# Starting a lane's next block under the old one's tail, and ScalarE steps ordered by activation table, in a four-layer graph kernel

## What is computed

```python
x = _layernorm(x + attention_gather_scatter(x, edge_attr, src, dst, ...))        # layer 0
x = _layernorm(x + L1(x, ...))                                                    # layer 1
x = _layernorm(x + segment_sum(x[col] * edge_attr[:, None], row) @ W.T + b)       # layer 2
x = _layernorm(x + segment_sum(value[:, None] * x[col], row))                     # layer 3

def L1(x, ...):
    att = segment_softmax(x[src] @ att_w[:D] + x[dst] @ att_w[D:], dst)
    messages = att[:, None] * (alpha * phys + (1.0 - alpha) * neur)
    h = _layernorm(gelu(segment_sum(messages, dst)) + x, ln1_g, ln1_b)
    m = gelu(h @ mlp_w1.T + mlp_b1) @ mlp_w2.T + mlp_b2
    return _layernorm(m + h, ln2_g, ln2_b)
```

## Time and profile before

| | us |
|---|---|
| median of 3 runs | 3338.48 (3337.09 to 3351.1) |
| the profiled execution | 3352.47 |
| its span in the profile | 3350.7 |
| busy: TensorE, VectorE, ScalarE, GpSimd | 2159.2, 1627.2, 1632.0, 2055.5 |

### The profile page before, as it was taken

How to read it: one execution, slowest core, us unless ns; L and a number is a source line. 1 busy time by engine, 2 the same in 40 slices (tenths; PEclk the granted TensorE clock), 3 DMA queues, 4 the chain that set the end, 5 groups by cost and what they waited for, 6 DMA issues and landing times. The chain is left out here.

```text
span 3350.7 us, 28393 instructions
## 1 busy us (share of the span) xinstructions
PE 2159.2 (64%) x9124; PEld 1081.8 (32%) x9124; DVE 1627.2 (49%) x3065; ACT 1632.0 (49%) x2292; POOL 2055.5 (61%) x1609
## 2 busy tenths in 40 slices
PE   6885777687787888888885744778777730012221
PEld 3432333265333336334333633333332210001210
DVE  5873899837878673443332676332233310012221
ACT  4763566434677672777773333656567720001110
POOL 6888888600488810466657888688800048788887
PEclk9997898769999896999997656888899965555555
DMA  2221222106322211244347342111111101112221
GB/s 57 63 67 43 54 56 53 48 21 191 89 46 43 43 37 47 79 104 106 105 102 160 82 110 69 44 37 38 37 52 38 38 23 14 14 31 57 62 56 26
DMA packets 251594, 204.24 MB, mean 61 GB/s; under 512 B 182627, under 2 KB 192167, under 8 KB 251446
## 3 DMA queue, kind: packets, MB, share of 16 engines
q1 hardware_dynamic: 164998, 154.80, 16.3%
q0 software_dynamic: 83200, 47.29, 8.7%
q10 hardware_dynamic: 3248, 0.34, 0.1%
HBM read 133.83 MB, written 79.64 MB: 64 GB/s over the span
## 5 line engine op out<-in xcount | busy, mean ns | idle before, releaser
L810 PE MATMUL ps<-wk 127*64 127x125 f32 x1200 | 121.0, 367 | 559.0 <-DVE wk L795 558.0
L2172 POOL DMA_INDIRECT stab<-wk,rank_i x200 | 243.1, 1215 | 313.5 <-issue 247.8
L483 ACT ACTIVATE b_s<-ps,vec 128x512 f32<-128x512 f32 (+1 forms) x444 | 297.1, 682 | 125.7 <-PE ps L480 71.4
L2169 POOL DMA_INDIRECT u<-x2tab,dpos_i x200 | 278.0, 1390 | 79.6 <-issue 77.8
L2169 POOL DMA_INDIRECT u<-x3tab,src_i x200 | 258.4, 1292 | 72.3 <-issue 72.3
L2169 POOL DMA_INDIRECT u<-in_x_dram,dst_i x200 | 263.9, 1320 | 61.0 <-issue 57.6
L2169 POOL DMA_INDIRECT u<-in_x_dram,src_i x200 | 249.3, 1246 | 73.5 <-issue 69.2
L810 PEld LDWEIGHTS ps<-wk 127*64 127x64 f32 x1200 | 96.3, 191 | 580.7 <-DVE wk L795 576.7
L2172 POOL DMA_INDIRECT out_dram<-e_c,dst_i x72 | 89.4, 1242 | 309.2 <-issue 309.2
L840 ACT ACTIVATE e_a<-ps 128x500 f32<-128x500 f32 x75 | 44.0, 586 | 456.7 <-PE ps L810 452.3
L2169 POOL DMA_INDIRECT e_b<-x0tab,dpos_i x72 | 91.7, 1274 | 244.0 <-issue 244.0
(11 more groups left out here) (416 smaller groups left out, 5653.5 us busy)
## 6 DMA issues: line engine op xcount, KB each, us to landing
b_s<-in_x_dram SPq DMA_DIRECT2D x98, 256.0 KB
out_dram<-b_gl SPq DMA_DIRECT2D x98, 256.0 KB
wk<-dlist SPq DMA_DIRECT2D x50, 500.0 KB
wk<-slist SPq DMA_DIRECT2D x50, 500.0 KB
u<-stab SPq DMA_DIRECT2D x25, 510.0 KB
x2none<-b_gl SPq DMA_DIRECT2D x25, 250.0 KB
wk<-x2none SPq DMA_DIRECT2D x25, 240.0 KB
x2tab<-wk SPq DMA_DIRECT2D x25, 240.0 KB
```

The source lines that it names most:

```text
L483: return nc.scalar.activation(b_s[l][:, 0:w], (pA, pB)[n][l][:, 0:w], ACT.Abs_reciprocal_sqrt, bias=col(EPSV))
L810: last_a = nc.tensor.matmul(e0[64 * (k % 2):64 * (k % 2) + 64, P * (k // 2):P * (k // 2) + P], msg[n % 2][0:P + 2, D * k:D * k + D], sr[n ...
L2169: pool.indirect_dma_start(out=o, out_offset=None, in_=tab, in_offset=at(ix), **kw).then_inc(s, 16)
L2172: pool.indirect_dma_start(out=tab, out_offset=at(ix), in_=a, in_offset=None, bounds_check=rows_n - 1, oob_is_err=False).then_inc(s, 16)
```

## The change

**The lane.** A dense block's x is now loaded into the second half of `b_gl` and already after `w2` of the lane's previous job (`mlp_pe`), the transposes `t` go to pB, `c` to pA and `j` to pB. So `t` waits only for the lane's last reciprocal root (`rstds`), `u` (or `x`) for the old block's `rows` (`rows_ps`), and `c` (`a`, `s`) for its `out` (`rows_out`). In the plan `-lane` moves from `out` to `r4` (source, destination) or `r5` (dense).

**The plan.** Square roots become a table of their own (3) and steps in no table keep what is loaded. ScalarE looks 1.5 us ahead (`SAME_TABLE`): among the steps that can begin by then, those that need no table change come first, whatever their rank. `GRACE` is .1 instead of .2, copies `act|dve` count each engine's slowness and table change, and `HOLD` starts no dense block in two stretches (before the first source group, and from late in layer 1's carried rows to the third destination group). No arithmetic changes.

```diff
+        LAST_MLP = MLP.format(" -lane")
+        MLP = MLP.format("")
...
-            unit(("src", g), 1, "t pe .5 +lane;x act 1.2;s pe 2.2;r act .7;h dve .9;" + MLP + "rows pe .5;out act|dve .7 -lane",
+            unit(("src", g), 1, "t pe .5 +lane;x act 1.2;s pe 2.2;r act .7;h dve .9;" + LAST_MLP + "rows pe .5;out act|dve .7",
...
-                 "sq5 act .75;j5 pe 1.2;r5 act .7;o dve .75;rows pe .5;out act|dve .7 -lane", [(("dense", n - 1), "t", 0)] if n else ())
+                 "sq5 act .75;j5 pe 1.2;r5 act .7 -lane;o dve .75;rows pe .5;out act|dve .7", [(("dense", n - 1), "t", 0)] if n else ())
...
-        TABLES = {"gelu": 1, "g": 1, "exp": 2}
+        TABLES = {"gelu": 1, "g": 1, "exp": 2, "r": 3, "r3": 3, "r4": 3, "r5": 3, "rs": 3, "rst": 3}
...
-        GRACE = .2
+        GRACE, X_IN, SAME_TABLE = .1, 6.0, 1.5
+        HOLD = ((("u3", 0, "t"), ("src", 0, "t")), (("lay", 1, "b10"), ("dst", 2, "t")))
+        HOLD = [((a[0:2], a[2]), (z[0:2], z[2])) for a, z in HOLD]
...
+            def lane_at(l, key):
+                return max(lane_free[l], x_free[l] if key[0] == "dense" else 0.0)
+
+            def slow(eng, t):
+                return next((f for a, z, f in BUSY if a <= t < z), 1.0) if eng == "dve" else 1.0
+
+            def switch(eng, name):
+                return 1.28 if eng == "act" and TABLES.get(name, table[0]) != table[0] else 0.0
...
                     if r == "lane":
-                        t = max(t, min(max(lane_free[l], lane_rows[l] + 6 if key[0] == "dense" else 0.0) for l in LANES))
+                        t = max(t, min(lane_at(l, key) for l in LANES))
+                        if key[0] == "dense" and any(a in end and z not in end for a, z in HOLD):
+                            t = 1e6
...
+                if "|" in units[key]["steps"][name][1]:
+                    t += (slow(eng, t) - 1) * units[key]["steps"][name][2] + switch(eng, name)
...
-                    pick = min((units[s_[0]]["rank"], t, s_, eng) for t, s_ in cand if t <= first + GRACE)
+                    wait = max(GRACE, SAME_TABLE) if eng == "act" else GRACE
+                    pick = min((switch(eng, s_[1]), t > first + GRACE, units[s_[0]]["rank"], t, s_, eng)
+                               for t, s_ in cand if t <= first + wait)[2:]
...
+                        names_ = list(units[key]["steps"])
+                        names_ = names_[names_.index("t"):]
+                        for k, p in ((1, "rows"), (2, "out")):
+                            if last[l] and (last[l], p) not in end:
+                                left[key, names_[k]] += 1
+                                then.setdefault((last[l], p), []).append((key, names_[k], 0.0))
+                        last[l] = key
...
+                if name == "w2":
+                    x_free[lane_of[key]] = done + X_IN
...
             if m:
-                pe.wait_ge(S(f"rows_out{l}"), m)
+                pe.wait_ge(S(f"rstds{l}"), c)
+            else:
+                pe.wait_ge(S("w_made"), 2)
             for q in range(4):
-                last_t = nc.tensor.transpose(pA[l][:, 128 * q:128 * q + 128], b_s[l][:, 128 * q:128 * q + 128], ident[:, :])
+                last_t = nc.tensor.transpose(pB[l][:, 128 * q:128 * q + 128], b_gl[l][:, 512 + 128 * q:640 + 128 * q], ident[:, :])
             last_t.then_inc(S(f"head_t{l}"), 1)
             yield t["c"]
             pe.wait_ge(S(f"head_u{l}"), before(l, m, dense=1) + 1)
-            nc.tensor.matmul(pB[l], blk_c[:, :], b_h[l][:, :], start=True, stop=True).then_inc(S(f"head_c{l}"), 1)
+            if m:
+                pe.wait_ge(S(f"rows_out{l}"), m)
+            nc.tensor.matmul(pA[l], blk_c[:, :], b_h[l][:, :], start=True, stop=True).then_inc(S(f"head_c{l}"), 1)
             yield t["j"]
             pe.wait_ge(S(f"squares{l}"), c + 1)
-            nc.tensor.matmul(pA[l], blk_j[:, :], b_s[l][:, :], start=True, stop=True).then_inc(S(f"means{l}"), 1)
+            nc.tensor.matmul(pB[l], blk_j[:, :], b_s[l][:, :], start=True, stop=True).then_inc(S(f"means{l}"), 1)
...
-            if on["dense", n, "u"] == "act":
+            c, o = squares_before(l, m), on["dense", n]
+            if o["u"] == "act":
                 yield t["u"]
                 act.wait_ge(S(f"head_t{l}"), m + 1)
-                nc.scalar.activation(b_h[l][:, :], pA[l], ACT.Identity, bias=col(B0)).then_inc(S(f"head_u{l}"), 1)
+                if m:
+                    act.wait_ge(S(f"rows_ps{l}"), m)
+                nc.scalar.activation(b_h[l][:, :], pB[l], ACT.Identity, bias=col(B0)).then_inc(S(f"head_u{l}"), 1)
...
-            yield max(t["t"] - 6, lane_jobs[l][m - 1][0]["rows"] + 1.2 if m else 0)
+            yield lane_jobs[l][m - 1][0]["w2"] + 2.4 if m else t["t"] - 6
             if m:
-                sp.wait_ge(S(f"rows_ps{l}"), m)
-            sp.dma_start(b_s[l][:, :], x[dense_row(n):dense_row(n) + NB, :].rearrange("(p t) d -> p (t d)", p=128)).then_inc(
+                sp.wait_ge(S(f"mlp_pe{l}"), 3 * m - 1)
+            elif l == 1:
+                sp.wait_ge(S("setup_ps"), 1)
+            sp.dma_start(b_gl[l][:, 512:1024], x[dense_row(n):dense_row(n) + NB, :].rearrange("(p t) d -> p (t d)", p=128)).then_inc(
```

More of the change, by code:

```diff
@@ L257, in gnn_resnorm_kernel @@
             sums_unit(NG + g, "msg dve 1.4;same dve 1.2;t pe .5 +lane;x act .6;a pe 2.2;ag act 1;o pe 1.2;g act .6;c pe 2.3;sq act .7;"
[L258 removed]
+                      "j pe 1.2;r act .7;h dve .75;" + LAST_MLP + "rows pe .5;out dve 1.3",
                       [(("lay", 1), "copy", CARRIED if g == 0 else 0)] + [(("xd1", g), "mul", 0)],
@@ L331, in make_plan @@
             spare = {"e0": START["pe"], "e1": START["pe"]}
-            lane_free, lane_rows, lane_of = [START["pe"] for _ in LANES], [-1e9 for _ in LANES], {}
+            lane_free, x_free, last, lane_of = [START["pe"] for _ in LANES], [-1e9 for _ in LANES], [None for _ in LANES], {}
             end, at_, jobs = {}, {k: {} for k in order}, [[] for _ in LANES]
+            on.update({k: {} for k in order})
             left, then, ready = {}, {}, {}
             opened = {e: [] for e in free}
-            table = [0]
+            table = [3]
             def open_if(key, name):
@@ L378, in make_plan @@
                 _, engs, us, takes, gives, _ = units[key]["steps"][name]
-                on[key[0], key[1], name] = eng
-                if eng == "dve":
-                    us *= next((f for a, z, f in BUSY if a <= t < z), 1.0)
-                if eng == "act" and TABLES.get(name, 0) != table[0]:
-                    table[0] = TABLES.get(name, 0)
-                    us += 1.28
+                on[key][name] = eng
+                if "|" not in engs:
+                    us = us * slow(eng, t) + switch(eng, name)
+                if eng == "act":
+                    table[0] = TABLES.get(name, table[0])
                 for e in engs.split("|"):
@@ L402, in make_plan @@
                         spare[r] = 1e9
-                if name == "rows" and key in lane_of:
-                    lane_rows[lane_of[key]] = done
+                if name == "w2":
+                    x_free[lane_of[key]] = done + X_IN
                 for r in gives:
@@ L570, in dense_act @@
                                  scale=1.0 + EPS).then_inc(S(f"rstds{l}"), 1)
-            if on["dense", n, "out"] == "act":
+            if o["out"] == "act":
                 yield t["out"]
@@ L590, in dense_dve @@
                                            ALU.mult).then_inc(S(f"dense_o{l}"), 1)
-            if on["dense", n, "out"] == "dve":
+            if o["out"] == "dve":
                 yield t["out"]
```

84 lines of the change are left out of this document (46 added, 38 removed).

## The result

| | before | changed |
|---|---|---|
| median, us | 3344.79 (3337.09 to 3353.3, 4 runs) | 3263.59 (3262.4 to 3270.59, 4 runs) |
| ratio, 95% interval | | 0.9761 (0.9728 to 0.9794) |
| span of the profiled execution, us | 3350.7 | 3268.8 |

What follows compares the result with a forecast made beforehand. A chain with waits, not any engine's busy time, was taken as the bound. -101 + 4 - 19 - 26 + 14 + 5 = -123 us against the profiled 3352.5, set against the median 3338.48, gave 3215 us; range 3158 to 3272.

Steps and rivals of the forecast that it cites:

- Blocks left at the end (-101): Dense blocks left behind layer 3's last gathers fall from 20.1 to 12.5; 7.6 at 13.3 us give -101 us.
- their pace (-19): Dense blocks left at the end come every 11.8 us instead of 13.3, over 12.5 blocks: -19 us.
- rival B: Only block counts help, paces stay 15.3 and 13.3 us; 3270 us; sign: j5 intervals at 13 or above; chance 0.17.
- The second softmax (+14): Softmax after the last x1s sum starts later, as VectorE has 70 instructions ahead instead of 45: +14 us.
- The first sums (+5): Stretch 767 to 864: about six more matmuls stand between the first and last sums, costing +5 us.
- Destination groups (-26): Groups pacing u4 come every 14.2 us instead of 15.3, by fewer loads and no rows-to-t wait: -26 us.
- rival C: Lanes fall into step in destination groups and dense rest, leaving TensorE idle; slower, 3393 us at p = 0.25; chance 0.06.
- +4: Allowance for TensorE reaching layer 3's last gather late, being about 85% busy in 2116 to 2434: +4 us.
- The table load: Each ScalarE load saved frees 1.3 us and no more; the skill's added drain of about 1380 ns was left out.

Runs made afterwards that it cites:

- e11: e7 with HOLD emptied, so dense blocks may begin anywhere; 3189.54 us, ratio 0.9546.
- e1: Changed kernel without ScalarE's table rule (lowest rank picked within GRACE), overlap and HOLD kept; 3188.85 us, ratio 0.9535.
- e8: e1 with the xd1 groups given rank 1 instead of 2, ahead of dense blocks; 3220.45 us, ratio 0.9626.
- e10: e1 with HOLD emptied, so dense blocks may begin anywhere; 3210.34 us, ratio 0.9601.
- e7: Changed kernel with SAME_TABLE 0.5 us instead of 1.5, a shorter look ahead for the table rule; 3182.1 us, ratio 0.9515.
- e5: Changed kernel with the table rule off from the end of the second softmax to the last destination group; 3231.53 us, ratio 0.9665.
- e13: Kernel before with only GRACE .1 and the plan's new table costs, no pick by table; 3345.75 us, ratio 0.9999.
- e6: Changed kernel with VectorE's compare of each destination group placed 3 us later in its order; 3253.65 us, ratio 0.9728.
- e2: Kernel before with the table rule (new tables, SAME_TABLE 1.5, GRACE .1) but no overlap of lanes; 3370.78 us, ratio 1.0073.
- e12: e7 with GpSimd's stages u1, u2 and u3 planned at 12.6 us a group instead of 12.2; 3173.92 us, ratio 0.9505.
- e3: Changed kernel planned with 8.0 us instead of 5.0 for an edge list to arrive, in all layers; 3197.51 us, ratio 0.9562.
- e9: e1 planned with 6.5 us instead of 5.0 for an edge list to arrive; 3198.82 us, ratio 0.9568.

## Why the prediction was right in direction and range, and wrong in one step

**Blocks left at the end (-101) and their pace (-19): right.** Forecast was a standstill of about 171 us, measured 172.5; j5 steps were to come every 11.8 us and came every 12.0 from the first to the last. By the forecast's own count, which begins at the last j5 ahead of the last group (2464.73, to 2632.40), it is 167.7 / 13 = 12.9, since 24 us pass before the first of them; so the pace was met by one count and nearly missed by the other (13 or above was the sign of rival B). What doesn't hang on the count is the remainder: 115 us less 101 for the blocks are 14, forecast were 19 less 4. One sum describes the table of runs: blocks left times pace, plus 20 us. It is bookkeeping more than a forecast, as the pace is measured in the same stretch. It is within 3 us in seven of the eleven kernels whose pace is given (before apart), and worst for e11, 9 us too low. The 20 us are before's 287.6 - 20.1 x 13.3, the chain from the last j5 to the first scatter and the entry into the stretch.

| | left x pace + 20 | measured |
|---|---|---|
| changed | 12.5 x 12.0 + 20 = 170 | 172.5 |
| e1 | 9.2 x 11.2 + 20 = 123 | 121.5 |
| e8 | 14.2 x 11.7 + 20 = 186 | 185.1 |
| e10 | 7.2 x 11.2 + 20 = 101 | 102.0 |
| e7 | 10.5 x 10.4 + 20 = 129 | 136.0 |

The attribution was off, however. The forecast counted the table loads saved in this stretch as part of the faster pace. e1, with all of them back, has the faster pace (11.2) and 3.3 blocks fewer left: so the loads are not where the gain comes from, and 3.3 x 12.0 + 9.2 x 0.8 = 47 of the 51 us between the two standstills are block count and pace. Whether the 0.8 is the rule's is open: e5, with the rule on in that stretch, has 11.1.

**The second softmax (+14): right in size.** The wait ahead of `u4` grew by 17. The last `x1s` sum and the softmax's steps, answering to the earlier trace rows; of line 1204 the second is the last start given, 1264.5:

```profile
1205.23 0.69 DVE L1025 TENSOR_TENSOR u<-u,e_b 125x512 f32<-125x512 f32 x1
```
```profile
L1204 DVE TENSOR_TENSOR score<-score,r5c x2: 347/357/367, 659.9 to 1264.5; 125x200 f32<-125x200 f32 x2
```

59 us pass, 21 more than before; forecast were 50 or so. e8 confirms the cause by taking it away. The prediction put the delay down to dense blocks and same-table steps; e13 has it too (+19) with neither overlap nor rule, so `GRACE` or the plan's table costs are enough for it.

**The first sums (+5): too small.** The wait ahead of `u3` grew by 10; e1 has none of it (221.1), so it belongs to the rule.

**Destination groups (-26): this step failed.** It read "the lane loses its wait from rows to t", put the pace midway between 15.3 and TensorE's 13.2, and gave the gain to `u4`. The steps did come a little faster, answering to the earlier trace rows:

```profile
L764 ACT ACTIVATE b_x<-ps x25: 578/587/588, 1358.2 to 1713.4; 128x500 f32<-128x500 f32 x25
```

That is 355.2 / 24 = 14.8 us, 11 us over 24 intervals instead of 26. But `u4` ends 62 us after the last of these steps instead of 49, so nothing of the 11 arrives. Two things went wrong. First, the wait that the overlap removes was no part of what paces these groups: e1 and e13 have the same `u4` to 0.7 us and nearly the same interval (14.4 and 14.6). The start times of groups 5 to 22 show where it went. From a group's `out` to the `t` of the group that follows it in its lane passed 2.9 us in e13 and -1.3 in e1 (`t` now comes first), 4.2 us gained; but a group's own way from `t` to `out` grew from 41.3 to 46.2 us, so that what was gained ahead of `t` was lost again between the group's own steps. Before and in the changed kernel it is 3.8 to -1.1 and 42.9 to 47.2. These groups also load no x through the lane, so the load that made up most of the dense blocks' 5.7 us was never in their way. Second, the loads saved were counted as time that the lanes get. Here is what they get instead, around 1508 and 1521 in the changed kernel:

```profile
1507.90 1.28 ACT L517 ACT_TABLE_LOAD   x1
1509.19 1.09 ACT L517 ACTIVATE b_gl<-ps,vec 128x1000 f32<-128x1000 f32 x1
...
1514.92 1.20 DVE L839 TENSOR_TENSOR wk<-wk,vcd 127x1000 f32<-127x1000 f32 x1 [3.48 <-DMA wk<-carried]
...
1520.27 0.74 DVE L536 SCALAR_TENSOR_TENSOR b_h<-ps,vec,b_s 128x500 f32<-128x500 f32 x1 [4.15 <-ACT b_s L509]
1521.32 0.74 DVE L536 SCALAR_TENSOR_TENSOR b_h<-ps,vec,b_s 128x500 f32<-128x500 f32 x1 [0.30 <-ACT b_s L509]
...
1523.28 1.38 DVE L540 SCALAR_TENSOR_TENSOR b_h<-ps,vec,b_x 128x500 f32<-128x500 f32 x2
1524.04 1.26 ACT L528 ACTIVATE b_s<-b_h 128x500 f32<-128x500 f32 x2 [1.45 <-DVE b_h L540]
...
1529.98 1.20 POOL L2216 DMA_INDIRECT stab<-wk,rank_i  x1 [9.71 <-DVE wk L807]
```

Two lanes take the same step one behind the other: two of line 536 after VectorE idled 4.15 us for ScalarE's root, two of line 540, two squares. Then GpSimd has idled 9.71 us for the rows of one group, and gets those of the second right after. That is what rival C describes, at a small size. How much of the rule's 75 and 25 us it carries is not shown, and the traces speak against the pairs alone: VectorE's wait for the root ahead of line 536 is 28.2 us between 1420 and 1700 here and 73.1 in e1, where the groups come evenly; and e7's dense blocks come in pairs at the fastest pace of all.

**A rival that was left out: TensorE's clock.** The granted clock of `u4` is 0.96 before and 0.95 in the changed kernel, and 0.97 in e6, 0.98 in e2, 0.99 in e13 and e7, 1.00 in e1, e5 and e12, all of which have a shorter `u4`. In the changed kernel it falls to the lower level for a few us at a time, several times over. One such fall, in the timeline and in two windows:

```profile
1497.51 2.03 PE L503 MATMUL ps<-b_h,wt 128*128 128x500 f32 x2 [4.60 <-DVE b_h L536]
```
```profile
1485.00:1495.00 10.00, 7.91 (x34) 3.30 (x33) 3.57 (x5) 8.20 (x10) 8.03 (x7) 1.00 0.69 188
1495.00:1502.00 7.00, 4.49 (x6) 1.99 (x7) 2.59 (x3) 1.62 (x2) 5.78 (x5) 0.53 0.34 81
```

TensorE had idled 4.60 us for line 536, and its pair of matmuls then took 2.03 us where such a pair takes 1.0 to 1.1 nearby. As an estimate from the clocks, 5% of 379 us, 19 us of full-speed time, were lost in the changed kernel's `u4` and next to none in e1's, against a difference of 15 us in length. In the dense stretch the clock is 0.91 (changed) and 0.98 (e1). So the rule may cost by letting TensorE stand, and then once more by the clock. No run parts the order from the clock, and the clock is not all of it: e10 and e3 have 0.99 and 1.00 in `u4` at lengths of 378.6 and 403.7.

**So the kernel gained 42 us less than forecast** (81 of 123). The time forecast, 3215, lies 49 us below the measured 3263.59; the other 7 us are the median of before, 3338.48 when the forecast was made and 3344.79 beside the result. By parts, forecast to measured: the standstill -116 to -115 (the forecast's -101, +4 and -19), `u4` -26 to -1, ahead of `u4` +14 to +17, ahead of `u3` +5 to +10, the rest 0 to +7. The destination groups are 25 of those 42.

**The table load.** One load and what follows it starts 1.29 us apart (1507.90 to 1509.19), as in the earlier trace rows. No drain of 1.38 us, which the prediction cites from the Trainium skill, shows behind it; in the median of the 323 loads of the kernel before that stand between two operations, 1.31 us pass from the end of the one to the start of the other. The Trainium skill (ScalarE: Activation LUTs, section "Table sets: the hidden batching unit") asks to batch activations by table set. In this kernel the runs with the full look ahead show the contrary: the square above has it cost 25 and 75 us, and the weaker form in e7 is neutral. ScalarE is busy for 81% of `u4` in e1, so it isn't simply idle; what the loads save there, the order that saves them gives back in waits of other engines.

**What stays open.** What sets the destination groups' interval at 14.4 and 14.6 us in e1 and e13 is not known: TensorE was busy for 240 of 280 us there in the changed kernel, which is 12.7 a group, and e12 gets to 13.6. Why e9 and e10 lengthen the wait ahead of `u4` was not traced instruction by instruction. And pairs were seen in the order and in the timeline; a version that breaks the pairs while it keeps the 218 loads was not tried, so which part of the 75 us the pairs carry, which the clock and which the blocks that the plan leaves for the end, is open.

## What to carry to other kernels

Price a change part by part on the stretch where a wait ends last: here the blocks left times their pace gave the standstill within 9 us in each variant with a pace, within 3 in most. Saved work on an engine that the stretch does not wait for is worth nothing by itself; ask what the order that saves it makes the others wait for, read each stretch's granted clock beside its busy time, and run the parts apart, since one half of this change (-157 us, `HOLD` and the copies included) hid the price of the other (+75). And work moved out of an idle stretch lands in another: in e3 and e8 a large part of what one stretch won, another gave back.
